# Unread multiplications around the last batch's turning and logits, and the other batches' logits one row tile back

## The chip, the core and the metric

The kernel runs on one core of one Trainium2 chip. The time is device microseconds of one launch; before the change the median of three runs is 2252.08 us (2251.83 to 2252.51). Engines are named as in the profile: PE is TensorE's matmul, PEld its weight load, DVE VectorE, ACT ScalarE, POOL GpSimd, SP SyncE.

## What is computed

Eight sequences of 768 tokens, 256 wide: 256 tokens from a state-space kernel of the input and 512 text tokens. Behind them one attention block and one mixture of experts, in 32-bit floats:

```python
h = _L0_tok_ref(L0_tok_log_dt, L0_tok_inv_A_real, L0_tok_A_imag, L0_tok_B_ri, x, 256)
h = jnp.concatenate([h, txt], axis=1)
h = h + _L0_attn_ref(_layernorm(h, axis=-1), Wq, Wk, Wv, Wo)
# the feed-forward part, on layernorm(h):
logits = xf @ Wr + br
topk_w, topk_idx = jax.lax.top_k(logits, TOP_K)      # 2 of 8 experts
topk_w = jax.nn.softmax(topk_w, axis=-1)
h1 = jax.nn.relu(jnp.einsum('th,ehf->etf', xf, W1) + b1[:, None, :])
y = jnp.einsum('etf,efh->eth', h1, W2) + b2[:, None, :]
out = jnp.einsum('te,eth->th', gate, y)
```

## The kernel before

It works in stages: the state-space kernel, attention, routing (`route`) and experts (`experts`). The change lies in routing, from 1594 to 1850 us of the profiled execution.

Routing goes through the eight batches one after the other. A batch has six row tiles (TT = 6) of 128 tokens. `loop` gives every engine the same shape: batch 0 written out, a loop of three passes with two batches each, batch 7 written out, then `drain`, which finishes batch 7.

PE, for each tile t of batch b: `project` waits for the attention rows (oT_in) and for the addition of three tiles earlier (h1_ready), then does 8 matmuls into bank t % 3 of A (L1023; the trace has two records for each matmul). The batch before is handled in between, at fixed tiles: behind tile TURN_AT = 1 `turn(b-1)` transposes the 12 blocks of the normalised rows (L1033), with tr_done after every four. In tile LOGITS_AT = 2 the logits of the six row tiles are put between the matmuls from the third on (L1042, two matmuls of 8 columns a tile); the first of them waits for xT_ready, that is for ACT's three copies (L1079) of what was turned. Behind tile COUNTS_AT = 3 `counts(b-1)` does two matmuls of the mask (L1051, L1052).

DVE, for each tile: `add` adds the projection to h (L1123) and takes the statistics of the tile before (L1126). `choose(b-1)` follows the addition of tile LOGITS_AT: it reads the logits (L1155), finds the best two and writes the mask (L1169). `place(b-1)` follows the addition of tile COUNTS_AT: from the counts it works out the slots and writes idx (L1194). At the batch's end `norm` makes the normalised rows xn (L1134 to L1148), for which the next batch's turn waits (xn_ready).

ACT copies what was turned, loads h of the batch after next behind it, does the exponential (L1083) and the square root (L1074) and stores h. SP loads the attention rows of the next batch and one expert's weights in each batch. POOL's `scatter` (L1000) sends each row tile's rows to the slots of its two experts: it waits for idx, then before every tile for the count h1_ready of `paced`; twelve indirect DMAs a batch.

In `drain` PE turns batch 7, does its 24 logit records in one go, then the counts. DVE chooses and places, writes tail_i and the tile table (`tile_table`, L1237 to L1256). SP waits for the table, fetches the first tile of expert rows (L1305) and weights (L1309), and the expert stage begins, whose first record on PE is L1336. Its loads wait for `placed`, which POOL raises when the scatters of batch 6, and then of batch 7, have landed.

Of the kernel before, what the change touches and what calls it, by code (L numbers as in the profile page):

```python
# [18 lines left out]
NB, SEQ, D = 8, 768, 256  # L19
# [4 lines left out]
TT = SEQ // P  # L24
# [23 lines left out]
def hold(eng, sem, value):  # L48

    eng.wait_ge(sem, value)  # L50
    eng.nop(nofuse=True)
# [847 lines left out]
def route(nc, block, sb, PS, sem, io, ident, img_d, oT_d, xs_d, acc_d, oT, oT_in, wo_in, h1, run, base, exp_i, src_i, tail_i, needs_i, held_by, adds_i, wo, wr, br, weights, weights_in, table_ready, adds_ready):  # L899
# [26 lines left out]
    A, XT, L = PS[:, 0:3], PS[:, 3:6], PS[:, 6]  # L926
# [5 lines left out]
    oT_free, h1_ready, var_ready, sd_ready, xn_ready = (sem(f"r_{n}") for n in ("oT_free", "h1_ready", "var_ready", "sd_ready", "xn_ready"))  # L932
# [4 lines left out]
    h_stored, tail_ready, placed = sem("r_h_stored"), sem("r_tail_ready"), sem("r_placed")  # L937
    norm_dve, pick_dve, place_dve = sem("r_norm_dve"), sem("r_pick_dve"), sem("r_place_dve")
    scattered = [sem(f"r_scattered{q}") for q in range(2)]
    TURN_AT, LOGITS_AT, COUNTS_AT = 1, 2, 3  # L940
    NORM, PICK, PLACE = 2 * TT + 4, 2 * TT + 4, TT + 7

    def loop(iteration, drain, eng):

        iteration(0, 0)
        with eng.Fori(0, (NB - 2) // 2) as k:
            iteration(k * 2 + 1, 1)
            iteration(k * 2 + 2, 0)
        iteration(NB - 1, 1)
        drain()  # L950
# [4 lines left out]
    @block.sync  # L955
    def _(sp):
        sp.nop().then_inc(oT_free, 3)

        assert NE == NB
        for b in range(NB):  # L960
            if b + 1 < NB:
                sp.wait_ge(oT_free, b * TT + 3)
                load_rows(sp, oT, oT_d, oT_in, b + 1, (b + 1) % 2)
            sp.dma_start(b1[:, b], io["b1"][b].rearrange("(c p) -> p c", p=P), allow_slow_non_contiguous=True).then_inc(weights_in, 16)
            sp.dma_start(w2[:, b], io["W2"][b].rearrange("(c p) f -> p c f", p=P)).then_inc(weights_in, 16)
            sp.dma_start(b2[:, b], io["b2"][b].unsqueeze(0).to_broadcast([P, D])).then_inc(weights_in, 16)
        sp.wait_ge(weights_in, 3 * NE * 16)
        sp.wait_ge(tail_ready, 1)
        for x in range(0, NE, 2):
            row = sp.value_load(tail_i[0:1, x:x + 1], min_val=x * STRIDE, max_val=x * STRIDE + TOK)  # L970
            sp.dma_start(xs_d[bass.ds(row, P), :], pads[:]).then_inc(zeroed[0], 16)
        sp.wait_ge(table_ready, 1)

    @block.gpsimd
    def _(pool):

        pool.memset(ones[:], 1.0).then_inc(const, 1)
        pool.wait_ge(const, 1)
        pool.affine_select(out=below[:], in_=ones[:], compare_op=ALU.is_gt, fill=0.0, base=0,
                           pattern=[[1, P]], channel_multiplier=-1).then_inc(const, 1)  # L980
        pool.iota(eight[:], [[1, NE]], base=0, channel_multiplier=0, allow_small_or_imprecise_dtypes=True).then_inc(const, 1)
        pool.iota(base[:], [[STRIDE, NE]], base=0, channel_multiplier=0, allow_small_or_imprecise_dtypes=True).then_inc(const, 1)
        pool.iota(tile_no[:], [[1, NT]], base=0, channel_multiplier=0, allow_small_or_imprecise_dtypes=True).then_inc(const, 1)
        pool.memset(pads[:], 0.0).then_inc(const, 1)
        pool.memset(xn[:, :, :, D + 5:DX], 0.0).then_inc(const, 1)
        pool.iota(tok_i[:], [[SEQ, NB], [P, TT]], base=0, channel_multiplier=1).then_inc(const, 1)
        pool.wait_ge(const, 6)
        pool.memset(pads[:, D + 1:D + 1 + TOPK], -2.0).then_inc(const, 1)
        pool.iota(pads[:, D:D + 1].bitcast(I32), [[0, 1]], base=TOK, channel_multiplier=1).then_inc(const, 1)
        pool.iota(pairs[:, 1:NT], [[16, NT // 2], [0, 2]], base=0, channel_multiplier=0, allow_small_or_imprecise_dtypes=True).then_inc(const, 1)  # L990
        pool.nop().then_inc(xn_free, 2)

        def scatter(b, k, q):
            hold(pool, idx_ready, b + 2)
            for t in range(TT):
                if not (isinstance(b, int) and b == NB - 1):
                    paced = (b + 1) * TT + COUNTS_AT + 4 + t
                    hold(pool, h1_ready, min(paced, NB * TT + 3) if isinstance(b, int) else paced)
                for e in range(TOPK):
                    pool.indirect_dma_start(out=xs_d, out_offset=bass.IndirectOffsetOnAxis(ap=idx[:, q, e, t:t + 1], axis=0),  # L1000
                                            in_=xn[:, q, t, :], in_offset=None).then_inc(scattered[q], 16)
            pool.wait_ge(scattered[q], k * (TT * TOPK * 16) + TT * TOPK * 16)
            if isinstance(b, int) and b >= NB - 2:
                if b == NB - 1:
                    for r in range(2):
                        pool.wait_ge(zeroed[r], 16 * (NE // 2))
                pool.nop().then_inc(placed, 1)
            else:
                pool.nop().then_inc(xn_free, 1)

        with pool.Fori(0, NB // 2 - 1) as k:
            for q in range(2):
                scatter(k * 2 + q, k, q)
        for q in range(2):
            scatter(NB - 2 + q, NB // 2 - 1, q)

    @block.tensor
    def _(pe):
        def project(b, q, t, beside=None):
            pe.wait_ge(oT_in[2 * q + t // 3], (b >> 1) * (KV * 16) + KV * 16)  # L1020
            pe.wait_ge(h1_ready, b * TT + t + 1)
            for c in range(KV * 2):
                last = pe.matmul(A[:, t % 3, 0:D], oT[:, q, c // 2, c % 2, P * t:P * t + P], wo[:, c, :], start=(c == 0), stop=(c == KV * 2 - 1))  # L1023
                if beside is not None and c >= KV * 2 - TT:
                    logits(beside, [c - (KV * 2 - TT)])
            last.then_inc(oT_free, 1)

        def turn(b, q):
            pe.wait_ge(xn_ready, b + 1)
            for n in range(3):  # L1030
                for m in range(4):
                    c, t = (4 * n + m) // TT, (4 * n + m) % TT
                    last = pe.transpose(XT[:, n, P * m:P * m + P], xn[:, q, t, P * c:P * c + P], ident[:])  # L1033
                last.then_inc(tr_done, 1)

        def logits(b, tiles):
            if 0 in tiles:
                pe.wait_ge(xT_ready, b * 3 + 3)
                pe.wait_ge(mask_ready, b + 1)
            for t in tiles:  # L1040
                for c in range(KC):
                    last = pe.matmul(L[:, NE * t:NE * t + NE], xT[:, c, P * t:P * t + P], wr[:, c, :], start=(c == 0), stop=(c == KC - 1))  # L1042
            if TT - 1 in tiles:
                last.then_inc(lg_done, 1)

        def counts(b):
            pe.wait_ge(const, 2)
            pe.wait_ge(mask_ready, b + 2)
            pe.wait_ge(idx_ready, b + 1)
            m = mask[:].rearrange("p t e -> p (t e)")  # L1050
            pe.matmul(C[:, 0].rearrange("p t e -> p (t e)"), below[:], m, start=True, stop=True)  # L1051
            pe.matmul(C[:, 1].rearrange("p t e -> p (t e)"), ones[:], m, start=True, stop=True).then_inc(count_done, 1)  # L1052

        def iteration(b, q):
            for t in range(TT):
                project(b, q, t, b - 1 if not first(b) and t == LOGITS_AT else None)
                if not first(b) and t == TURN_AT:
                    turn(b - 1, 1 - q)
                if not first(b) and t == COUNTS_AT:
                    counts(b - 1)  # L1060

        def drain():
            turn(NB - 1, 1)
            logits(NB - 1, range(TT))
            counts(NB - 1)

        pe.wait_ge(wo_in, 16)
        loop(iteration, drain, pe)

    @block.scalar  # L1070
# [383 lines left out]
def program(nc, x, txt, log_dt, inv_A_real, A_imag, B_ri, Wq, Wk, Wv, Wo, Wr, br, W1, b1, W2, b2, rotary, out):  # L1454
# [6 lines left out]
    with ExitStack() as ctx:  # L1461
# [33 lines left out]
        with nc.Block() as block:  # L1495
            placed, h_stored = route(nc, block, sb, PS, sem, io, ident, img_d, oT_d, xs_d, acc_d, oT, oT_in, wo_in, h1, run, base, exp_i, src_i, tail_i, needs_i, held_by, adds_i, wo, wr, br, weights, sem("weights_in"), table_ready, adds_ready)
            experts(nc, block, sb, PS, sem, io, ident, xs_d, acc_d, exp_i, src_i, needs_i, held_by, adds_i, weights, placed, h_stored, table_ready, adds_ready)
# [32 lines left out]
```

## Time and profile before

| | |
|---|---|
| median of three runs | 2252.08 us |
| profiled execution | 2256.4 us |
| its span | 2254.4 us |
| PE, PEld | 2051.4 us (91%), 1240.2 us (55%) |
| DVE, ACT, POOL | 1771.6, 1071.3, 875.4 us |
| mean granted TensorE clock | 0.977 |

The page cuts the span into 40 slices of 56.4 us; each digit is a busy share in tenths, 9 is 90% or more. PEclk is the granted TensorE clock, in tenths of full speed.

```profile
PE   0469999999999999999999999988899959999998
DVE  8889999999999999999999999998244443444443
PEclk9999999999999999999999999999998969999999
```

The clock has two levels, 2.4 GHz (1.00) and 1.2 GHz (0.50); a value between them is the mean of a stretch. Ends of matmuls are modelled, so what counts on PE is when a record starts.

### The profile page before, as it was taken

Reading aid. Unit: us, or ns where it says so; the run is one execution under the profiler, and the core shown is the slowest. Engines: PE = TensorE matmul, PEld = TensorE weight load, DVE = VectorE, ACT = ScalarE, POOL = GpSimd, SP = SyncE. Lnnn points to the kernel's source line nnn. Section 1 sums busy time; section 2 is a strip of 40 time slices with the busy share of each in tenths; the row PEclk is TensorE's granted clock in tenths of the full one; section 3 lists DMA queues with packets and bytes.
Section 4 is the critical chain, followed back from the end, with each engine's and each line's share of the span. In section 5 each row is a group of like instructions: output and inputs, shape, how many; then the busy total and the mean of one; then the engine's idle time right before and its main releaser. Section 6 shows DMA issues by size and latency. Waiting matters only on the chain. (4 is left out here: it accounts for less than half of the span.)

```text
span 2254.4 us, 59220 instructions
## 1 busy us (share of the span) xinstructions
PE 2051.4 (91%) x21098; PEld 1240.2 (55%) x21099; DVE 1771.6 (79%) x3227; ACT 1071.3 (48%) x2463; POOL 875.4 (39%) x831
## 2 busy tenths in 40 slices
PE   0469999999999999999999999988899959999998
PEld 0334444444444444444444444433688849999997
DVE  8889999999999999999999999998244443444443
ACT  2145556555655656556655665564111113444443
POOL 0026424444364344542642444230033443444443
PEclk9999999999999999999999999999998969999999
DMA  2145354443644544445435534543675638898985
GB/s 61 41 108 128 106 128 116 124 121 98 151 107 103 150 112 121 118 109 139 117 104 128 122 106 121 126 122 119 215 250 193 229 125 219 209 213 208 213 209 137
DMA packets 189542, 317.02 MB, mean 141 GB/s; under 512 B 48913, under 2 KB 127121, under 8 KB 189329
## 3 DMA queue, kind: packets, MB, share of 16 engines
q1 hardware_dynamic: 156640, 275.39, 45.0%
q0 software_dynamic: 19440, 25.58, 6.2%
q10 hardware_dynamic: 13248, 13.13, 1.7%
q8 instruction: 144, 2.36, 0.5%
q14 instruction: 70, 0.57, 0.1%
HBM read 214.75 MB, written 92.31 MB: 136 GB/s over the span
## 5 line engine op out<-in xcount | busy, mean ns | idle before, releaser
L767 ACT ACTIVATE a_prob<-ps_s,a_nmax 128x768 f32<-128x768 f32 x768 | 685.7, 897 | 577.2 <-DVE a_nmax L852 577.2
L852 DVE TENSOR_REDUCE a_nmax<-ps_s 128x1 f32<-128x768 f32 x768 | 694.3, 943 | 47.9 <-PE ps_s L693 42.7
L858 DVE STREAM_TRANSPOSE a_probT<-a_prob 128x768 f32<-128x768 f32 x768 | 700.4, 950 | 1.1 <-ACT a_prob L767 1.1
L693 PE MATMUL ps_s<-a_kT,a_qT 64*128 64x384 f32 x3072 | 612.3, 512 | 55.1 <-ACT a_prob L767 51.5
L700 PE MATMUL ps_o<-a_probT,a_vrep 32*64 32x384 f32 x12288 | 561.2, 491 | 6.5 <-DVE a_probT L858 5.0
L693 PEld LDWEIGHTS ps_s<-a_kT,a_qT 64*128 64x128 f32 x3072 | 258.8, 185 | 390.4 <-ACT a_prob L767 274.6
L829 POOL TENSOR_TENSOR a_o<-a_o,a_invrow 128x1536 f32<-128x1536 f32 x32 | 110.0, 3438 | 791.3 <-ACT a_o L775 791.3
L700 PEld LDWEIGHTS ps_o<-a_probT,a_vrep 32*64 32x64 f32 x12288 | 243.5, 132 | 293.5 <-issue 129.7
L498 POOL TENSOR_TENSOR a_prod<-a_raw,a_table 128x384 f32<-128x384 f32 x304 | 294.2, 1000 | 132.3 <-ACT a_raw L759 128.9
L1409 POOL DMA_INDIRECT out_dram<-e_y,e_row_i x103 | 160.5, 1558 | 231.9 <-DMA out_dram<-e_y,e_row_i 145.7
L1346 PE MATMUL ps_r<-e_xT,e_w 128*128 128x128 f32 x1648 | 202.0, 276 | 0.0
L1023 PE MATMUL ps_r<-wo,r_oT 128*128 128x256 f32 x768 | 192.4, 404 | 9.1 <-DVEq L1214 9.1
L1353 PE MATMUL ps_r<-ew,e_hT 128*128 x824 | 194.7, 379 | 0.0
L1346 PEld LDWEIGHTS ps_r<-e_xT,e_w 128*128 128x128 f32 x1648 | 193.5, 193 | 0.1
L1384 ACT ACTIVATE e_hT<-ps_r,e_b_now 128x128 f32<-128x128 f32 x412 | 117.5, 368 | 159.9 <-PE ps_r L1346 104.6
L679 PE MATMUL ps_o<-a_xT,wq 128*128 128x384 f32 x512 | 185.8, 501 | 0.0
L1023 PEld LDWEIGHTS ps_r<-wo,r_oT 128*128 128x128 f32 x768 | 149.4, 201 | 28.5 <-issue 9.7
L1000 POOL DMA_INDIRECT xs_d<-r_xn,r_idx x96 | 93.2, 970 | 166.0 <-DVE h L1123 131.5
L1353 PEld LDWEIGHTS ps_r<-ew,e_hT 128*128 128x128 f32 x824 | 148.8, 190 | 16.0
L767 ACT ACTIVATION_READ_ACCUMULATOR a_prob<-ps_s,a_nmax 128x1 f32 x768 | 151.2, 197 | 0.0
L679 PEld LDWEIGHTS ps_o<-a_xT,wq 128*128 128x128 f32 x512 | 91.0, 189 | 88.9 <-issue 25.6
L1427 DVE TENSOR_TENSOR e_y<-ps_r,eb 128x256 f32<-128x256 f32 x103 | 43.8, 425 | 105.7 <-PE ps_r L1353 98.7
(221 smaller groups left out, 1301.2 us busy)
## 6 DMA issues: line engine op xcount, KB each, us to landing
e_w<-in_L_ffn_W_dram SPq DMA_DIRECT2D x103, 512.0 KB
a_qT<-q_d SPq DMA_DIRECT2D x124, 384.0 KB, 8.9
a_vrep<-v_d SPq DMA_DIRECT2D x128, 192.0 KB, 3.8
a_invrow<-inv_d SPq DMA_DIRECT2D x64, 384.0 KB, 5.2
oT_d<-a_o SPq DMA_DIRECT2D x32, 768.0 KB, 3.2
r_oT<-oT_d SPq DMA_DIRECT2D x64, 384.0 KB
q_d<-a_qp SPq DMA_DIRECT2D x31, 768.0 KB, 3.7
e_x<-xs_d SPq DMA_DIRECT2D x103, 132.0 KB
```

The source lines that it names most:

```text
L498: eng.tensor_tensor(scratch[n], a, f, ALU.mult).then_inc(done, 1)
L679: last = pe.matmul(X[:, 0:HALF], w, xn[:, k, HALF * c:HALF * c + HALF], start=(k == 0), stop=(k == KC - 1))
L693: last = pe.matmul(S[:, s % 2, r, 0:HALF], qT[rows, par, 2 * hp + c, P * t:P * t + P], kT[rows, par, :], start=True, stop=True)
L700: last = pe.matmul(O[DH * c:DH * c + DH, q, 0:HALF], vrep[rows, j % NQ, j // NQ, :], keys(par, c, j, rows), start=(j == 0), stop=(j == NJ ...
L767: act.activation(prob[:, s % RING, :].rearrange("p (r k) -> p r k", r=2), S[:, s % 2, :, 0:HALF], ACT.Exp, bias=nmax[:, s % RING:s % RING ...
L852: v.tensor_reduce(nmax[:, s % RING:s % RING + 1], S[:, s % 2, :, 0:HALF], AX.XY, ALU.max, negate=True).then_inc(max_ready, 1)
L858: v.transpose(turned(par, s), prob[:, s % RING, :]).then_inc(t_ready, 1)
L1023: last = pe.matmul(A[:, t % 3, 0:D], oT[:, q, c // 2, c % 2, P * t:P * t + P], wo[:, c, :], start=(c == 0), stop=(c == KV * 2 - 1))
L1346: last = pe.matmul(H[:, q, P * f:P * f + P], w1[:, n, c, P * f:P * f + P], xT[:, q, P * c:P * c + P], start=(c == 0), stop=(c == KC - 1))
L1353: last = pe.matmul(Y[:, q, 0:D], hT[:, q, P * c:P * c + P], w2[:, bass.ds(ex, 1), c, :], start=(c == 0), stop=(c == FC - 1))
L1384: last = act.activation(hT[:, q, P * f:P * f + P], H[:, q, P * f:P * f + P], ACT.Relu, bias=b1_now[:, n, f:f + 1], scale=1.0)
L1409: pool.indirect_dma_start(out=acc_d, out_offset=bass.IndirectOffsetOnAxis(ap=row_i[:, n:n + 1], axis=0), in_=y[:, n, :], in_offset=None, c ...
```

## The change

LOGITS_AT goes from 2 to 3 and COUNTS_AT from 3 to 4, for all engines; POOL's `paced` has 3 in place of 4, which gives the same count as before. In PE's `drain` come a wait for h1_ready and matmuls into bank 0 of A (256 columns, the identity as the stationary operand, wo as the moving one) that nobody reads: 13 ahead of the turn, 2 ahead of the logits, 5 ahead of the counts.

```diff
@@ -937,7 +937,7 @@
-    TURN_AT, LOGITS_AT, COUNTS_AT = 1, 2, 3
+    TURN_AT, LOGITS_AT, COUNTS_AT = 1, 3, 4
@@ -994,7 +994,7 @@
-                    paced = (b + 1) * TT + COUNTS_AT + 4 + t
+                    paced = (b + 1) * TT + COUNTS_AT + 3 + t
@@ -1059,9 +1059,17 @@
+        def warm(count):
+            for _ in range(count):
+                pe.matmul(A[:, TT % 3, 0:D], ident[:], wo[:, 0, :], start=True, stop=True)
+
         def drain():
+            pe.wait_ge(h1_ready, NB * TT + 1)
+            warm(13)
             turn(NB - 1, 1)
+            warm(2)
             logits(NB - 1, range(TT))
+            warm(5)
             counts(NB - 1)
```

## Rows read from the trace of the kernel before

**Rows 1.** Windows: start:end and length, busy us (records) of each engine, clock, DMA.

```profile
core 0: us, PE busy (x) PEld busy (x) DVE busy (x) ACT busy (x) POOL busy (x), PEclk, DMA share, GB/s
1624.63:1650.02 25.39, 25.39 (x137) 22.55 (x136) 13.24 (x72) 4.56 (x7) 6.06 (x6) 1.00 0.69 225
1650.02:1676.36 26.34, 25.43 (x138) 22.51 (x137) 13.09 (x72) 4.77 (x7) 11.75 (x13) 1.00 0.78 267
1676.36:1710.15 33.79, 32.09 (x137) 27.86 (x136) 13.02 (x72) 4.56 (x7) 11.50 (x13) 0.80 0.61 207
1710.15:1742.39 32.24, 30.41 (x137) 26.63 (x136) 13.00 (x72) 4.56 (x7) 11.53 (x13) 0.84 0.64 216
1742.39:1772.90 30.51, 28.76 (x138) 25.24 (x136) 13.00 (x72) 4.56 (x7) 11.52 (x13) 0.89 0.68 230
1772.90:1800.09 27.19, 25.43 (x138) 22.55 (x137) 13.05 (x72) 4.56 (x7) 11.45 (x13) 1.00 0.81 276
...
1818.50:1837.00 18.50, 9.17 (x41) 8.54 (x40) 8.30 (x52) 3.49 (x6) 9.49 (x10) 0.57 0.36 123
```

**Rows 2.** Timeline: start, us, engine, line, operation [idle before, releaser]; turns of batches 5, 6.

```profile
1772.90 1.47 PE L1033 MATMUL ps_r<-ident,r_xn 128*128 128x128 f32 x12
...
1775.80 0.60 ACT L1079 ACTIVATE r_xT<-ps_r 128x512 f32<-128x512 f32 x1 [7.36 <-PE ps_r L1033]
1775.85 0.42 DVE L1123 TENSOR_TENSOR h<-ps_r,h 128x256 f32 x1 [3.98 <-remote]
...
1777.43 0.61 PE L1042 MATMUL ps_r<-wr,r_xT 128*128 128x8 f32 x4 [1.76 <-ACT r_xT L1079]
...
1800.09 1.47 PE L1033 MATMUL ps_r<-ident,r_xn 128*128 128x128 f32 x12
...
1800.72 1.57 ACT L1079 ACTIVATE r_xT<-ps_r 128x512 f32<-128x512 f32 x3 [5.08 <-DVE h L1123]
...
1802.69 0.51 PE L1042 MATMUL ps_r<-wr,r_xT 128*128 128x8 f32 x4
...
1803.57 0.51 PE L1042 MATMUL ps_r<-wr,r_xT 128*128 128x8 f32 x4
```

**Rows 3.** Timeline: from the last batch's turn to the first expert tile.

```profile
1824.26 2.82 PE L1033 MATMUL ps_r<-ident,r_xn 128*128 128x128 f32 x12 [5.75 <-DVE r_xn L1148]
...
1827.76 5.29 PE L1042 MATMUL ps_r<-wr,r_xT 128*128 128x8 f32 x24 [0.69 <-ACT r_xT L1079]
...
1829.77 0.96 POOL L1000 DMA_INDIRECT xs_d<-r_xn,r_idx  x1 [0.30 <-issue]
1833.09 0.21 DVE L1155 TENSOR_TENSOR r_lg<-ps_r,br 128x48 f32<-128x48 f32 x1 [8.89 <-PE ps_r L1042]
...
1835.84 0.64 PE L1051 MATMUL ps_r<-r_mask,r_below 128*128 128x48 f32 x2 [2.79 <-issue]
...
1849.02 0.38 SPq L1305 DMA_DIRECT2D e_x<-xs_d  x1
...
1851.51 0.69 PE L1336 MATMUL ps_r<-ident,e_x 128*128 128x128 f32 x2 [14.61 <-DMA e_x<-xs_d]
```

**Rows 4.** A window of 1 us behind the last projection, columns as in rows 1.

```profile
1821.00:1822.00 1.00, 0.00 (x0) 0.00 (x0) 0.86 (x5) 0.00 (x0) 0.88 (x1) 0.58 0.78 250
```

**Rows 5.** Timeline of PE: projections at the half and at the full clock.

```profile
1689.91 6.14 PE L1023 MATMUL ps_r<-wo,r_oT 128*128 128x256 f32 x16
...
1786.20 14.05 PE L1023 MATMUL ps_r<-wo,r_oT 128*128 128x256 f32 x64
```

**Rows 6.** Timeline of DVE: normalised rows of batch 6, choosing and placing in batch 7.

```profile
1796.76 2.03 DVE L1148 TENSOR_SCALAR r_xn<-h,r_mv,r_s 128x256 f32 x6
...
1807.96 0.19 DVE L1155 TENSOR_TENSOR r_lg<-ps_r,br 128x48 f32<-128x48 f32 x1
...
1811.19 0.42 DVE L1123 TENSOR_TENSOR h<-ps_r,h 128x256 f32<-128x256 f32 x1 [0.51 <-issue]
...
1815.09 0.42 DVE L1123 TENSOR_TENSOR h<-ps_r,h 128x256 f32<-128x256 f32 x1
```

## The prediction

> **What bounds the kernel now.** I read the busy slices of the page first. The routing stage (1594 to 1850 us) is slices 29 to 33: PE falls to 5 in the last of them, and the clock to 8 in slice 31 and 6 in slice 33. In the expert stage behind it PE stands at 9 up to the last slice. Then I cut the routing stage at the starts of the turns, one row a batch [rows 1]. The reader is to see that a period of the loop takes 25.39, 26.34, 33.79, 32.24, 30.51 and 27.19 us for the same 137 or 138 matmul records. Period minus PE's busy time is PE's pause: 0, 0.91, 1.70, 1.83, 1.75 and 1.76 us. The granted clock is 1.00 in three periods and 0.80, 0.84 and 0.89 in the others. So TensorE is the bound, and loses time in two ways: it pauses, and it then runs at 1.2 GHz instead of 2.4. DMA is at 0.81 or less and POOL is busy under 12 us a period; no record of the projections (L1023) in the loop is shown waiting.
>
> The timeline of one period says where the pause is [rows 2]. The turn starts at 1772.90, ACT begins the copies of it at 1775.80, 2.90 us later, and PE stands from the end of three matmuls of tile 2 until the logits start at 1777.43. In the last period ACT starts 0.63 us after the turn and nothing waits. DVE's add of tile 1 is late at the same moment (idle 3.98 us, released by "remote"); this repeats in four periods. Why PE's signals arrive late there no row says.
>
> After the last projection (1818.50) a second stretch begins in which little overlaps [rows 1, 3]: DVE normalises, PE turns at 1824.26 and does 24 logit records from 1827.76, DVE chooses from 1833.09, counts at 1835.84, SP fetches the first expert tile at 1849.02, PE takes it at 1851.51. The clock falls shortly after 1821 us, some 2.9 us after the last projection [rows 4], so turn, logits and counts run at 1.2 GHz. Behind it the expert stage is PE-bound (the digits of 9 in the page) and moves as a whole: what the table gains, the end gains.
>
> **Logits one tile back.** Nothing is added or removed on PE; 24 records lie in tile 3 instead of 2. PE now reaches the first logits after the turn (12 records, 1.31 us), all of tile 2 and three matmuls of tile 3. A projection record at the full clock is 14.05/64 = 0.2195 us [rows 5], a tile of 16 is 3.51, three matmuls are 1.32: together 6.1 us after the turn's start. The copies are done at 2.90 + 1.57 = 4.5 us at the latest seen (1.57 being the three copies of the last period). The pause should go from all five periods, with 1.6 us to spare: 0.91 + 1.70 + 1.83 + 1.75 + 1.76 = 7.95 us.
> The clock follows, I think. The six periods sum to 175.46 us; six of the undisturbed 25.39 are 152.34. The difference, 23.12 us, holds the pauses and 15.17 us of slow clock, all of it behind pauses of 1.70 us or more. The two passes without a pause (the first period and the last batch, same interleaving of logits) kept 1.00. I take the whole 23.1. The bounds are 7.95 (the clock falls regardless) and 23.1; I take the upper since every row without a pause lies there. A denser loop asks DMA for the same work in 25.4 us; the first period carried it.
>
> What moves with it: DVE chooses after add 3 and places after add 4. Choosing took 1807.96 to 1811.19, 3.23 us; add, statistics and placing took 1811.19 to 1815.09, 3.90 us [rows 6]. In the frame of the last batch, projection 3 ends at 1811.1: add 3 at 1811.2, statistics 0.35 + 0.34, choosing to 1815.1 (projection 4 ends 1814.7), add 4, placing, add 5 at 1819.0 in place of about 1818.55. So each normalisation comes some 0.5 us later. In the loop this is covered: the last of the normalised rows was ready at 1798.8 by the row of 2.03 us in [rows 6], the turn began at 1800.09, so 1.3 us of cover become 0.8 and turning does not wait. In the last batch it is bare: +0.5 us. The mask is ready at about 1814.5, projection 4 ends at 1814.7, so counts wait for nothing; without that luck it is 0.1 us a batch.
> On POOL the threshold is (b+1)*6+7+t before and after; only the index comes 3.7 us later, so four scatters go out together. A scatter is 0.96 us and 0.30 idle [rows 3], a batch 12 x 1.26 = 15.1 us in 25.4: covered. The last but one batch's scatters, issued up to 1830.7 now, will end near 1834.5, ahead of the last index. ACT and SP wait on the same counts as before.
>
> **The multiplications in the drain.** The new wait is on add 3, done before projection 5 ends, so nothing stands behind it. 13 matmuls are 26 records x 0.2195 = 5.7 us, from 1818.55 to 1824.25; the normalised rows come at 1824.25 + 0.5 = 1824.7. They fill the wait, cost nothing and leave a gap of 0.5 us. The clock should be at 2.4 GHz at the turn.
> The Trainium skill (TensorE: Matmul & The Clock Gate, Back-to-back issue gap) gives 262 cycles for a warm matmul of 256 columns, 0.109 us. By it the 13 would be over in 2.8 us and leave 3.4 us idle, more than the clock survived in [rows 4], and the drain would gain nothing. The row has twice that for each of two records, so I go by the row.
> Turn: ACT starts 0.63 us behind it and copies in 1.57, 2.2 us in all [rows 2]; PE fills this with 1.31 + 4 x 0.2195 = 2.19 us, no delay. Logits: two groups start 0.88 us apart with two projection records between [rows 2], so a record is (0.88 - 0.44)/4 = 0.11 us and 24 are 2.64, against 5.29 now. From the turn to DVE's first read it was 1833.09 - 1824.26 = 8.83; it becomes 2.25 + 2.64 + 0.15 = 5.0. Gain 3.8. The five matmuls (2.2 us) lie inside choosing (2.7 us to the mask); faster counts give 0.1. Net of the 0.5: **3.4 us**.
> If the clock falls in there, logits return towards 5.29 and the five matmuls take 10 x 0.384 = 3.8 us ([rows 5], 6.14/16), 1.1 us past the mask: the net gain is then 0 to 2. Nothing in the drain reads the bank, and DVE's table, SP's pads and the first fetch are unchanged, so the gain arrives at 1851.51. The wait behind it for the last batch's scatters falls at the fourth expert tile, over 10 us after they were issued.
>
> **Sum.** 2256.4 - 23.1 - 3.4 = 2229.9 for a profiled execution. The runs' median, 2252.08, is 4.3 us below the profiled one. If that is a constant of profiling, the median will be 2225.6; if the runs lose 4.3 us less to the clock, it will be 2252.1 - 22.2 = 2229.9. No row decides; I take the middle, 2227.6.
>
> **Rivals.**
> A. The clock falls in the loop without a pause. For: the logits are records of 8 columns, and three periods lost up to 6.7 us this way. Against: both passes without a pause. Gain 7.95 + 3.4, with up to half of the 15.2: 2233 to 2241, about 2238.
> B. The wait moves to tile 3. PE's late signals came within 0.2 us of its pause in four periods, as if they waited for PE to stand; then ACT begins when PE stands again, 6.1 us after the turn. Against: in the second period the pause was half as long. Gain is the drain alone: 2248.7.
> C. The clock falls in the drain, over transposes and narrow logits. Gain 23.1 + 1: 2230 by the same middle. The Trainium skill (the same page, PE-mode transpose) says that the full clock does not engage for transposes. In the trace they ran at 1.00 in the loop, where dense projections stood on both sides; in the drain they don't.
> D. Slower. As B, but the pause, now behind tile 2, drops the clock in all five periods as it did in the third: 5 x 6.7 = 33.5 us instead of 15.2, +18.3 less 3.4: 2267. It decides itself where the signals come: later than 4.5 us after the turn's start and the pause is back.
>
> **Chances.** Forecast 0.60 (2225 to 2231), A 0.14, B 0.08, C 0.13, D 0.05. What a measurement of this kernel can tell from no change is about 0.2%, 4.5 us: B is "same" (0.08), D slower (0.04 to 0.05), the others faster (0.87). The range reaches from 2223 (the constant offset and some us that the shorter loop saves elsewhere) up to A's upper end, 2242; B and D stay outside.
>
> **What would show it.** Periods of 25.4 to 25.5 us with the granted clock at 1.00; no idle of the logits on ACT's copies; a turn near 5.7 + 0.5 us after the last projection, DVE's first read 5.0 us behind it; the first expert tile 26.5 us earlier. Wrong would be: logits of tile 3 with idle before them (B, D), periods above 27 without idle (A), 5 us of logit records in the drain (C), or turning that waits for normalised rows.

## The result, and the profile after

The changed kernel took 2276.18 us (median of four runs, 2269.63 to 2280.27) against 2251.95 us for the kernel before: 1.0105 times as long, 95% interval 1.0078 to 1.0131. 2227.6 us was forecast. The profiled execution took 2280.07 us, its span is 2278.1. The traces of both kernels show a lateness of TensorE's signals: what waits for a matmul starts some us after it. The traces of e1 to e8, on one chip, have it too; those on two other chips (e9, e10 and r1, r2) do not. On one of these the same change makes the kernel faster by 0.14%.

The page of the changed kernel, busy tenths and clock in 40 slices of 57 us:

```profile
PE   0479999999999999999999999987999859999998
DVE  8889999999999999999999999995334443444443
PEclk9879999999999999999999999999988869999999
```

Against the page of before, the clock is at 8 in three slices of the routing stage, where it was in one. The windows from turn to turn, as in [rows 1], the last but one up to the last projection and the last up to the first expert tile:

```profile
core 0: us, PE busy (x) PEld busy (x) DVE busy (x) ACT busy (x) POOL busy (x), PEclk, DMA share, GB/s
1627.33:1652.62 25.29, 25.29 (x138) 22.55 (x137) 13.12 (x72) 4.56 (x7) 4.36 (x5) 1.00 0.66 209
1652.62:1688.90 36.28, 32.09 (x137) 27.87 (x136) 13.20 (x72) 4.66 (x7) 11.90 (x13) 0.81 0.58 201
1688.90:1716.02 27.12, 25.87 (x138) 22.53 (x137) 13.14 (x72) 4.56 (x7) 11.47 (x13) 1.00 0.75 253
1716.02:1743.02 27.00, 25.80 (x137) 22.53 (x136) 13.07 (x72) 4.56 (x7) 11.55 (x13) 1.00 0.75 256
1743.02:1778.30 35.28, 31.82 (x137) 27.79 (x136) 13.24 (x72) 4.67 (x7) 11.45 (x13) 0.81 0.59 199
1778.30:1812.23 33.93, 30.43 (x137) 26.53 (x136) 13.16 (x72) 4.66 (x7) 11.56 (x13) 0.85 0.64 222
1812.23:1839.88 27.65, 24.70 (x105) 21.60 (x104) 7.88 (x50) 4.57 (x6) 7.07 (x8) 0.75 0.12 43
1839.88:1876.41 36.53, 15.81 (x81) 13.35 (x79) 17.92 (x91) 3.38 (x6) 20.39 (x21) 0.70 0.37 127
```

Only the first period is what was forecast. The others have pauses of 4.19, 1.25, 1.20, 3.46 and 3.50 us (length minus PE's busy time), where [rows 1] had 0.91 to 1.83. Three of them are longer than any before, with the clock at 0.81 to 0.85 in their periods; the two short ones cost no clock. From the first projection to the last it is 242.7 us instead of 223.9, and from there to the first expert tile 36.4 instead of 33.0. The first projection of the profiled execution came 2.7 us later than before, which no part of the change touches.

Where the second period's time goes is in its timeline (start, length, engine, line, operation, idle before it and what released it):

```profile
1652.62 1.47 PE L1033 MATMUL ps_r<-ident,r_xn 128*128 128x128 f32 x12
...
1657.46 0.96 POOL L1000 DMA_INDIRECT xs_d<-r_xn,r_idx  x1 [0.30 <-issue]
1657.71 0.60 ACT L1087 ACTIVATE r_xT<-ps_r 128x512 f32<-128x512 f32 x1 [9.54 <-remote]
...
1658.73 0.96 POOL L1000 DMA_INDIRECT xs_d<-r_xn,r_idx  x1 [0.30 <-issue]
1661.89 0.60 ACT L1087 ACTIVATE r_xT<-ps_r 128x512 f32<-128x512 f32 x1 [3.59 <-remote]
...
1662.22 0.42 DVE L1131 TENSOR_TENSOR h<-ps_r,h 128x256 f32 x1 [7.89 <-remote]
...
1663.03 0.66 PE L1042 MATMUL ps_r<-wr,r_xT 128*128 128x8 f32 x4 [4.19 <-ACT r_xT L1087]
```

The transposes were over at 1654.1, tile 2's projection at 1658.8, but ACT began at 1657.71 and DVE's addition of tile 2 at 1662.22. Both are released by "remote": the profile finds no instruction that ended then. In [rows 2] the same word stood at one addition, 3.98 us. POOL issues ten scatters in a row, from 5.6 us ahead of the turn to 7.1 us behind it. One signal comes through among them, at 1657.71; the rest come 2.2 us after the last has ended.

In the drain it is the logits' signal that is late. Answer to [rows 3]:

```profile
1845.49 1.49 PE L1033 MATMUL ps_r<-ident,r_xn 128*128 128x128 f32 x12
...
1848.63 2.98 PE L1042 MATMUL ps_r<-wr,r_xT 128*128 128x8 f32 x24 [0.78 <-issue]
...
1854.76 0.96 POOL L1000 DMA_INDIRECT xs_d<-r_xn,r_idx  x1 [0.30 <-issue]
1858.01 0.21 DVE L1163 TENSOR_TENSOR r_lg<-ps_r,br 128x48 f32<-128x48 f32 x1 [12.61 <-remote]
...
1860.76 0.63 PE L1051 MATMUL ps_r<-r_mask,r_below 128*128 128x48 f32 x2 [5.35 <-issue]
```

Turn and logits ran at 2.4 GHz but for the last 0.4 us (24 records in 2.98 us, before 5.29), and were over at 1851.6. DVE read them 6.4 us later, 2.3 us behind the last scatter.

### The profile page after: what moved, and what is told of

Its sections match the earlier page's. It is cut to its first block and busy times, and to the rows that moved or that the text cites. A ratio compares the mean times of both kernels' runs of the same rounds, so it can differ in the third digit from the quotient of the medians.

```text
span 2278.1 us, 59300 instructions
## 1 busy us (share of the span) xinstructions
PE 2078.5 (91%) x21138; PEld 1259.1 (55%) x21139; DVE 1772.6 (78%) x3227; ACT 1071.6 (47%) x2463; POOL 875.2 (38%) x831
## 5 line engine op out<-in xcount | busy, mean ns | idle before, releaser
L693 PE MATMUL ps_s<-a_kT,a_qT 64*128 64x384 f32 x3072 | 619.6, 518 | 51.2 <-ACT a_prob L767 47.6
L1023 PE MATMUL ps_r<-wo,r_oT 128*128 128x256 f32 x768 | 200.0, 414 | 11.4 <-DVEq L1222 9.0
L1131 DVE TENSOR_TENSOR h<-ps_r,h 128x256 f32 (+1 forms) x48 | 20.2, 422 | 135.0 <-PE ps_r L1023 81.2
```

Of the source, the lines that this page charges most:

```text
L693: last = pe.matmul(S[:, s % 2, r, 0:HALF], qT[rows, par, 2 * hp + c, P * t:P * t + P], kT[rows, par, :], start=True, stop=True)
```

## The experiments

**e1, only the logits moved.** In `drain` the wait and the three groups of unread multiplications are taken out.

```diff
-            pe.wait_ge(h1_ready, NB * TT + 1)
-            warm(13)
             turn(NB - 1, 1)
-            warm(2)
             logits(NB - 1, range(TT))
-            warm(5)
```

> Only the move of logits and counts by one tile; no unread multiplications. Theory S (scatters): PE's signals reach ACT and DVE late while POOL issues its scatters without a break, and the move makes the breaks go, because the index comes later and four scatters are released at once. Then the loop loses its 19 us here too (after: 242.6 us from the first projection to the last, before: 223.9) and the run takes 2252 + 19 = 2271 us. Rival W (the unread multiplications cause the loss): 2252 or less, about 2229 by the prediction.

Measured 2270.10 us (2267.57 to 2273.39), 1.0085 times before (1.0054 to 1.0117), as theory S expected. The loss is in the move of the logits. In its trace the loop, from the first projection to the last, took 229.1 us and not 242.6: single traces spread. But the ranges do not meet. With the logits where they were and the scatters untouched the loop took 217.2 to 226.9 us on this chip (e2, the kernel before, e6), with the logits moved 229.1 to 242.7 (e1, e4, the changed kernel). e1's drain, from the last projection to the first expert tile, is 36.2 us, 3 us longer than before too: the index comes later, the scatters now lie under the last logits, and DVE read those 12.3 us behind the turn, not 8.8.

**e2, only the unread multiplications.**

```diff
-    TURN_AT, LOGITS_AT, COUNTS_AT = 1, 3, 4
+    TURN_AT, LOGITS_AT, COUNTS_AT = 1, 2, 3
-                    paced = (b + 1) * TT + COUNTS_AT + 3 + t
+                    paced = (b + 1) * TT + COUNTS_AT + 4 + t
```

> Only the unread multiplications in the drain; logits and counts where they were. Theory S: the loop is as before. In the drain the scatters of batch 6 run until about 12.2 us behind the last projection and signals are released some 2 us behind them, so DVE reads the logits some 14.5 us behind the last projection, as before: 2252, within 2 us. The prediction's drain: DVE reads 10.8 us behind it, 2248. Rival W: slower by 3 us or more.

Measured 2257.10 us (2252.28 to 2266.22), 1.0026 times before (1.0008 to 1.0044). That is 6 us slower, within rival W's range; with e1's 19 us it makes up the 24 us of the changed kernel, so the unread multiplications cost time here too, but the smaller part. The drain took 40.4 us, worse than theory S and the prediction had it. Its last turn and that of the kernel before are the cleanest pair of all: the scatters lie at the same places around the turn (they start from 8.4 us ahead of it to 5.5 behind) as in [rows 3]. There PE stood idle ahead of the turn and ACT began 1.15 us after it. Here PE multiplied until the turn, and the first copy began 7.14 us after it (turn at 1819.48):

```profile
1825.00 0.96 POOL L1000 DMA_INDIRECT xs_d<-r_xn,r_idx  x1 [0.30 <-issue]
```
```profile
1826.62 0.60 ACT L1087 ACTIVATE r_xT<-ps_r 128x512 f32<-128x512 f32 x1 [10.56 <-remote]
```
```profile
1829.21 5.29 PE L1042 MATMUL ps_r<-wr,r_xT 128*128 128x8 f32 x24 [7.33 <-ACT r_xT L1087]
```

PE waited 7.33 us, the clock fell, and the logits took the 5.29 us of the cold drain after all. Scatters alone do not make signals late, a busy PE alone neither (first period). Here it took both. Both are not always enough. The turns of batches 5 and 6 in the kernel before [rows 2] have scatters at the same places up to 1 us behind them and projections on both sides, and yet copies began 2.90 us behind the one and 0.63 behind the other. One thing that differs is DMA. Its share is the last but one number in these windows of 3 us behind a turn: first those two turns, then the turns of batches 6 and 7 in this experiment, prompt and late:

```profile
1772.90:1775.90 3.00, 2.77 (x19) 2.26 (x17) 0.05 (x1) 0.10 (x1) 1.67 (x2) 1.00 1.06 391
1800.09:1803.09 3.00, 3.00 (x24) 2.85 (x22) 0.76 (x2) 2.35 (x4) 2.39 (x3) 1.00 0.24 90
```
```profile
1795.33:1798.33 3.00, 3.00 (x24) 2.84 (x22) 0.76 (x2) 2.34 (x4) 2.39 (x3) 1.00 0.25 90
1819.48:1822.48 3.00, 2.40 (x16) 1.94 (x16) 0.00 (x0) 0.00 (x0) 2.09 (x4) 1.00 0.40 142
```

With scatters and projections beside it, a turn had late copies where DMA was at 1.06 and prompt ones where it was at 0.24 and 0.25. At 0.40, behind 26 unread records, they were later still, so a full DMA is not needed. What part it has is not shown.

**e3, scatters apart.** The changed kernel with one threshold altered: tiles 0 to 2 of a batch are scattered as soon as the index is there, tiles 3 to 5 only behind the addition of tile 3 of the next batch.

```diff
-                    paced = (b + 1) * TT + COUNTS_AT + 3 + t
+                    paced = (b + 1) * TT + (COUNTS_AT + 3 if t < 3 else TT + 7)
```

> The changed kernel with another threshold for the scatters: row tiles 0 to 2 go as soon as the index is there, tiles 3 to 5 only after the addition of tile 3 of the next batch, so that hardly a scatter is issued from the turn to the end of the logits in the loop. Theory S: the pauses go and the clock stays up; periods of 25.4 to 26 us, first to last projection some 202 us, 2252 - 22 + up to 3 in the drain = 2230 to 2234. Theory D (the lateness comes from a saturated DMA alone) and theory P (signals come when PE stands): periods above 30 us remain, 2265 or more.

Measured 2245.31 us (2243.22 to 2249.11), 0.9974 times before (0.9962 to 0.9987) and 1.4% under the changed kernel, but above the 2230 to 2234 of theory S. Windows of the second to fourth period:

```profile
1651.54:1677.92 26.38, 25.46 (x138) 22.42 (x136) 13.09 (x72) 4.66 (x7) 11.15 (x12) 1.00 0.78 254
1677.92:1704.17 26.25, 25.38 (x137) 22.56 (x137) 13.17 (x73) 4.56 (x7) 10.89 (x13) 1.00 0.81 266
1704.17:1730.59 26.42, 25.38 (x137) 22.55 (x137) 13.21 (x73) 4.78 (x7) 12.14 (x13) 1.00 0.81 269
```

No wait for the copies is left, the clock stays at 2.4 GHz in all periods, and the loop takes 205.5 us. Copies still begin up to 4.3 us behind the turn, beside scatters of which the last starts 1.1 to 2.3 us behind it; the cover of 6.1 us holds that. PE does not stand meanwhile, which rules out theory P. The 0.85 to 1.05 us of idle that remain in a period lie ahead of the turn, which waits for the normalised rows; their last addition is late by "remote" as well, and on the other chips this idle is absent (e9, e10). The clock did not fall over it. The drain, where all twelve scatters lie under PE's work, took 38.7 us, 5.7 more than before where 3 were allowed; the loop saved 18.4 us, not 22. The rest of the distance to 2232 is in the start: the trace with these 22 us was of an execution of 2256.4 us, 4 to 5 above the medians of its kernel.

**e4, the weights early.** The changed kernel, with SP's loads of all experts' second weights and biases moved into batch 0.

```diff
+            if b == 0:
+                for w in range(NB):
-            sp.dma_start(b1[:, b], ...
-            sp.dma_start(w2[:, b], ...
-            sp.dma_start(b2[:, b], ...
+                    sp.dma_start(b1[:, w], ...
+                    sp.dma_start(w2[:, w], ...
+                    sp.dma_start(b2[:, w], ...
```

> The changed kernel, all experts' second weights and biases loaded in batch 0, so that no weight load lies beside turns and scatters from the third batch on. Theory D (saturated DMA): the pauses of the later periods go, 2235 or less. Theory S: scatters are as in the changed kernel, so pauses of 3 us or more remain in most periods, 2262 to 2280, the attention rows of batch 2 perhaps late by some us in addition.

Measured 2274.36 us (2255.51 to 2280.67), 1.0082 times before (1.0053 to 1.0111). Periods of 34 us remain with DMA at 0.53 and 0.56:

```profile
1653.96:1687.97 34.01, 30.41 (x138) 26.64 (x136) 13.21 (x72) 4.77 (x7) 11.91 (x13) 0.85 0.53 174
1687.97:1721.95 33.98, 30.41 (x137) 26.64 (x136) 13.20 (x72) 4.67 (x7) 11.48 (x13) 0.85 0.56 190
```

The weight loads are not the cause. Theory D as a whole is not decided by this: the loads of the next batch's rows stayed, and in the 3 us behind the turn at 1687.97 DMA was at 1.07 all the same.

**e5, the drain apart too.** As e3; of batch 6's scatters the last six wait for the last logits.

```diff
                     hold(pool, h1_ready, min(paced, NB * TT + 3) if isinstance(b, int) else paced)
+                if isinstance(b, int) and b == NB - 2 and t == 3:
+                    hold(pool, lg_done, NB)
```

> As e3, and of batch 6's twelve scatters the last six wait for the end of the last logits. Theory S: the loop stays at 205.5 us; in the drain the copies and the logits go through while POOL is silent, DVE reads the logits some 5 to 6 us behind the turn (e3: 13.0), from the last projection to the first expert tile 29.5 to 31 us (e3: 38.7, before: 33.0), in all 2235 to 2238. If lateness has another source the drain stays at 36 us or more: 2243 to 2246.

Measured 2244.35 us (2242.20 to 2246.86), 0.9946 times before (0.9922 to 0.9970). The ratio is lower than e3's because the kernel before was slower beside e5 to e8 (2247 to 2272 us, median 2258.7) than beside e1 to e4 (2251.03); against e3's 2245.31 it is 1 us. DVE read the logits 5.2 us behind the turn at 1811.78, where the forecast has 5.0:

```profile
1816.98 0.21 DVE L1165 TENSOR_TENSOR r_lg<-ps_r,br 128x48 f32<-128x48 f32 x1 [5.26 <-PE ps_r L1044]
```

The releaser has its name again. The drain was 32.1 us, against 29.5 to 31 expected: the turn came 7.9 us behind the last projection, since the last addition had waited 2.1 us for "remote". The total did not reach 2235: the stage behind the first expert tile took 406.3 us instead of 402.0 in e3. In its first 20 us PE was busy 13.4 us at a clock of 0.60 (e3: 16.1 at 0.76). Why is not shown. Batch 7's scatters ended 6.8 us behind the first expert tile, 2.5 later than in e3; but e6, whose scatters ended as in e3, had 405.7 us too, and e9, whose scatters ended at 6.7, had 401.0.

**e6, wide multiplications.** As e2, with 512 columns and 6, 1 and 2 multiplications in place of 13, 2 and 5.

```diff
-                pe.matmul(A[:, TT % 3, 0:D], ident[:], wo[:, 0, :], start=True, stop=True)
+                pe.matmul(A[:, TT % 3, :], ident[:], wo[:, 0:2, :].rearrange("p a d -> p (a d)"), start=True, stop=True)
```

> As e2, the unread multiplications of 512 columns in place of 256: 6, 1 and 2 in place of 13, 2 and 5, about the same busy time in less than half the instructions. Theory R (what is held back grows with the number of PE's instructions beside the scatters): the copies begin 1 to 4 us behind the last turn (e2: 7.1), the drain is 33 to 37 us (e2: 40.4), 2247 to 2252. Theory B (it grows with PE's busy time or its reads): 7 us and 40 us again, 2257.

The drain took 34.5 us (e2: 40.4), the copies began 0.69, 2.34 and 5.18 us behind the turn (e2: the first at 7.14), with 12 records in 5.3 us ahead of the turn in place of 26 in 5.8. In this one trace the lateness went with the number of PE's instructions more than with its busy time. PE's idle ahead of the turn differs as well, 0.58 us against 0.12 in e2, and in e3, with 26 records of 256 columns and 1.67 us of idle behind them, the copies of the last turn were prompt (0.69 us), so the number is not shown to be what counts. The time of the whole, 2267.98 us (2251.34 to 2272.55), 1.0016 times before (0.9982 to 1.0049), says nothing: its loop, untouched by the edit, took 227 us in this trace and 217 in e2's, and the kernel before spread from 2247 to 2272 in the same comparison. The spread itself is a finding: the kernels with scatters apart (e3, e5, e7) stayed within 6 us.

**e7, apart and cold.** As e5 without the wait and the unread multiplications (the edit of e1).

> As e5 without the unread multiplications. The last turn, logits and counts run at 1.2 GHz: DVE reads 8.8 us behind the turn, 3.8 us later than in e5; the drain 33 to 34 us, 3 to 4 us above e5. If the clock's part of the prediction was wrong, the same time as e5.

Measured 2247.04 us (2245.42 to 2249.66), 0.9952 times before (0.9933 to 0.9970), against e5's 2244.35 in the same comparison; the drain 35.6 against 32.1 us. DVE read 8.8 us behind the turn, 3.6 later than in e5, where the forecast has 3.8. The clock's part of the forecast holds where signals are prompt.

**e8, scatters apart, logits near.** The kernel before with another threshold alone.

```diff
-                    paced = (b + 1) * TT + COUNTS_AT + 4 + t
+                    paced = (b + 1) * TT + (COUNTS_AT + 4 if t < 3 else TT + 6)
```

> The kernel before with only the scatters moved: tiles 0 to 2 as soon as the index is there, tiles 3 to 5 after the addition of tile 2 of the next batch. Theory S: the six scatters end over 2 us ahead of the turn, signals come 0.6 us behind it, the pauses and slow clock of the loop go: periods of 25.4, loop 202 us (before 223.9), 2230 us. If the move of the logits is what took the pauses away in e3, pauses of 1.7 us stay here, 2248 or more.

Measured 2248.18 us (2244.38 to 2250.58), 0.9947 times before (0.9922 to 0.9972). Theory S wanted 2230; by the total alone the rival, that the move of the logits took the pauses away in e3, would stand. The loop took 210.3 us and is a comparison in itself, since the scatters did not keep clear of every turn. The turn at 1712.27 came 1.7 us behind the end of the last scatter, that at 1680.60 in the middle of it:

```profile
1709.63 0.96 POOL L1000 DMA_INDIRECT xs_d<-r_xn,r_idx  x1 [0.31 <-issue]
```
```profile
1712.90 1.57 ACT L1079 ACTIVATE r_xT<-ps_r 128x512 f32<-128x512 f32 x3 [5.09 <-PE ps_r L1033]
```
```profile
1680.11 0.96 POOL L1000 DMA_INDIRECT xs_d<-r_xn,r_idx  x1 [0.30 <-issue]
```
```profile
1682.98 0.60 ACT L1079 ACTIVATE r_xT<-ps_r 128x512 f32<-128x512 f32 x1 [6.76 <-PE ps_r L1033]
```

The one began copying after 0.63 us and had a period of 25.16 us, the other after 2.38 us, with a pause of 1.24 us, the clock at 0.84 and 31.67 us. Three periods were free of pauses (the first has no scatters), three had 1.19 to 1.45 us. Setting the scatters apart took 13.6 of the 24 us that the loop loses (223.9 against 199.7 in r2) without moving the logits.

**e9 and e10** ran on another chip. e9 is e3 with e6's wide multiplications, e10 is e3 without any.

> As e3 (clean loop, scatters of batch 6 beside the drain), with the unread multiplications of e6: 512 columns, 6, 1 and 2 of them. Theory R (the lateness grows with PE's instructions beside the scatters): DVE reads the logits 8 to 11 us behind the last turn (e3: 13.0), the drain is 34 to 37 us (e3: 38.7) and the run 2242 to 2244. Theory B (with busy time or reads): as e3, 38 to 39 us.

> As e3 without the unread multiplications. Copies are on time because PE stood ahead of the turn; the end of the logits, a burst of 24 records under the last scatters, is signalled 1 to 4 us late as in e1 (DVE reads at 12.3 there). Drain 36 us, so the unread multiplications cost 2 to 3 us under scatters where they gain 3 apart from them (e5 against e7).

Both expectations were beside the point: no signal was late, with scatters beside every turn but the first. The copies began 0.64 us behind every turn in the loop and 0.69 in e9's drain (1.15 in e10's, at half the clock), the loops took 199.5 and 199.7 us, and the kernel before 2233.02 us. e9 took 2229.36 us (0.9981, 0.9971 to 0.9990), e10 2233.45 (0.9999, 0.9990 to 1.0009); the drains 29.0 and 32.6 us. Whether the number of instructions matters could not be tested again there.

**r1 and r2**, the changed kernel and the kernel before once more, on a third chip.

> The changed kernel once more, beside the kernel before. In e9 and e10, on another chip than e1 to e8, no signal of PE was late under scatters and the kernel before took 2233 us. If the lateness belongs to the chip, then on a chip without it the changed kernel has periods of 25.2 us, a loop of 199.7 us and a drain of 28 to 29 us, and is faster than the kernel before by the cold drain alone, 4 us (2229 against 2233); on a chip with it 2270 to 2280 against 2251.

> The kernel before, for its trace on the same chip as r1. Without the lateness copies begin 0.6 us behind every turn, pauses and slow clock are absent from the loop, which takes 199 to 201 us, and the drain 32 to 33 us. With it the trace is that of the kernel before as read for the prediction.

The changed kernel took 2229.93 us (2226.04 to 2231.22), 0.9986 times the kernel before (2233.22; 0.9976 to 0.9995); r2 is the kernel before itself, at 1.0006 (0.9996 to 1.0017). Two periods of r2, then of r1:

```profile
1649.01:1674.17 25.16, 25.16 (x137) 22.59 (x136) 13.13 (x72) 4.56 (x7) 11.66 (x13) 1.00 0.82 273
1674.17:1699.34 25.17, 25.17 (x138) 22.55 (x137) 13.18 (x72) 4.56 (x7) 11.39 (x13) 1.00 0.85 282
```
```profile
1650.16:1675.46 25.30, 25.30 (x138) 22.55 (x137) 13.11 (x72) 4.56 (x7) 12.05 (x13) 1.00 0.82 277
1675.46:1700.62 25.16, 25.16 (x138) 22.63 (x137) 13.23 (x72) 4.56 (x7) 11.33 (x13) 1.00 0.83 279
```

PE is busy throughout and at the full clock in both; the loops took 199.7 and 199.5 us. From the second turn on, r1's twelve scatters lay in a row from 5.6 us ahead of each turn to 9 us behind it, longer than in the first trace, and did no harm; nor did DMA, at 1.07 in the 3 us behind the turn at 1700.62. Its drain:

```profile
1799.96 1.48 PE L1033 MATMUL ps_r<-ident,r_xn 128*128 128x128 f32 x12
...
1802.23 2.85 PE L1042 MATMUL ps_r<-wr,r_xT 128*128 128x8 f32 x24
...
1823.40 0.69 PE L1344 MATMUL ps_r<-ident,e_x 128*128 128x128 f32 x2 [14.92 <-DMA e_x<-xs_d]
```

DVE read the logits 5.15 us behind the turn, and the drain took 28.9 us against 33.0 in r2.

## Why the prediction was wrong

*What bounds the kernel.* TensorE, its pauses and its clock: right for the trace that was read. But the pauses were taken for a property of the kernel. They are absent in r2, the same kernel on another chip, at 2234 us. The 23.1 us that the forecast wanted to win exist only where signals are late.

*The step that failed* is this one: "The copies are done at 2.90 + 1.57 = 4.5 us at the latest seen". It took the lateness as a fixed 2.9 us though no row explained it, and asked only for cover. The runs showed a lateness that depends on where the scatters lie. In four periods of the kernel before POOL had to stop at its thresholds soon after the turn, and the copies began 0.9 us behind the end of the last scatter. The move brought the index 3.5 us later (r1 against r2) and released up to ten scatters in one run across the turn; the first copies began 4.3 to 6.5 us behind it, the last up to 9.8, and a cover of 6.1 us was too small. Why scatters hold PE's signals back is open.

*The two clean passes* that the forecast leaned on were no witnesses for the others. The first period had no scatter beside its turn (POOL busy 6.06 us in [rows 1], 11.5 to 11.75 in the rest), and so had not "carried" the DMA of a denser loop either; the last pass had scatters beside its turn, but DMA at 0.24 behind it, where the four late ones had 1.06.

*The moved scatters* were seen ("four scatters go out together") and dismissed as "covered", because only POOL's own time was weighed, 15.1 us in 25.4. What they do to others was not. e3 altered nothing but their place and took 31 us off the changed kernel's 2276.

*Rivals B and D* named the right trigger, signals later than 4.5 us after the turn's start, and D's 2267 is 9 us from the result; it had 0.05. D's pauses dropped the clock in three of the five periods, and in the last batch. The sign that spoke for both, signals within 0.2 us of PE's pause, was a coincidence of another kind: POOL's pause lay there too, and in e3 signals came while PE ran. What should have raised their chance was that the forecast's whole gain hung on a lateness without a cause.

*The clock.* Right in the main. No period without a wait for the copies lost clock, in e3, e5, e9, r1 or r2; rival A fell. The bound of 1.70 us for a pause that costs clock was not one: a pause of 1.24 us was followed by the slow clock in e8 (0.84), pauses of 1.25 and 1.20 us in the changed kernel and one of 2.42 in e1 were not. And by the trace the clock fell 2.7 us behind the last projection, not 2.9. Rival C fell as well: in r1's drain turn and logits ran at the full clock, 1.48 and 2.85 us. The Trainium skill (TensorE: Matmul & The Clock Gate, PE-mode transpose) says that the full clock does not engage for transposes; here it stayed at 1.00 over the twelve, with unread multiplications on both sides, and the measurement decides.

*The drain.* Right on chips without lateness: 33.0 to 28.9 us, 4.1 gained where 3.4 were forecast. The terms: turn to DVE's read 5.15 us (forecast 5.0), and the delay of 0.5 us by the later placing did not come at all, since in r1 placing was over at 1794.47, before the last projection ended at 1794.51; the turn starts 5.4 us behind the last projection, against 5.7 before. In the first trace it failed by the same lateness: DVE read 12.5 us behind the turn.

*The price of a projection record*, taken from the row, was right: 26 records took 5.78 us and reached the normalised rows (PE idle 0.2 us at most in the changed kernel). The 0.109 us of the Trainium skill (TensorE: Matmul & The Clock Gate, Back-to-back issue gap) is half of the 0.22 us that a record took.

## What to carry to other kernels

A wait whose releaser is late without a reason ("remote" in the profile) is no fixed delay: find what goes on beside it, and find out whether it belongs to the kernel or to the chip, before an edit is built on it. Here the same two kernels compare at 1.0105 with the lateness and at 0.9986 on a chip without it. A pass that is free of the wait is a witness only if everything that runs beside the others runs beside it too. When an index or flag comes later, look at what its consumer queued up and will now issue in one burst, and at whose signals that burst lies upon. Multiplications into an unread bank ahead of a short chain do pay, 3 to 4 us here (e5 against e7, r1 against r2), as long as the signals behind them are prompt.

## What the runs showed of the hardware

On the chip of e1 to e8, and in the first two traces, semaphore signals of TensorE reached ScalarE and VectorE late while GpSimd issued indirect DMAs (0.96 us each, one every 1.26 us) beside a busy TensorE. Some came through among these, most 0.9 to 2.3 us after the last had ended. Several signals then came at once: the late copies often followed each other 0.5 us apart, as prompt ones do. It was not so at every such turn (batch 6 in the kernel before, e2 and e6, with copies 0.64 us behind). PE itself went on. In the changed kernel's fourth period it had issued 27 matmul records since the turn began when it stopped, in the middle of a tile, for want of nothing that the profile names:

```profile
1717.33 3.73 PE L1023 MATMUL ps_r<-wo,r_oT 128*128 128x256 f32 x15
1722.09 1.67 PE L1023 MATMUL ps_r<-wo,r_oT 128*128 128x256 f32 x7 [1.04 <-issue]
```

The Trainium skill (TensorE: Matmul & The Clock Gate, the table at its head) gives TensorE a queue of 64. The 27 records are 54 instructions with their weight loads; but in the fifth and sixth periods PE began 34 records, 68 instructions, ahead of the first copy. So no run here shows that a full queue stopped it.

Two other chips showed nothing of it, one of them with the same two kernels. What stays open: what in those chips differs, or in the state that they were in, since each of the two others was used once; what part the DMA load has; whether a scatter's issue or its packets hold the signals back, and whether the profiler, which recorded every execution compared here, has a part in it. That the number of PE's instructions counts (e6) rests on one trace.
